# Feed-forward tiles, key and query stages and row statistics at other steps of a software-pipelined Flamingo block, with its maximum jobs in another order

## What is computed

```
x = x + tanh(g_xattn) * attention(layernorm(x), ctx, ctx)     # 16 heads of 32, masked: ki <= qi + 1601 - 512
x = x + tanh(g_ffn)   * ffn(layernorm(x))                     # both sides rounded to fp8 by rows
  ffn: g, u = q(x) @ Wgate.T, q(x) @ Wup.T   (width 1408, by down_reorder_index)
       t = silu(g) * u ;  y = q(t) @ Wdown.T
```

## Time and profile before

| | us |
|---|---|
| median of 3 runs (1201.39 to 1202.09) | 1202.0 |
| the profiled execution | 1203.17 |
| its span | 1201.4 |
| PE busy | 1003.3 (84%) |
| DVE busy | 855.0 (71%) |
| ACT busy | 652.1 (54%) |
| POOL busy | 327.4 (27%) |

### The profile page before, as it was taken

One profiled execution on the slowest core, in us unless ns is written; L12 is line 12 of the kernel. 1 busy time (PEld: TensorE's weight loads), 2 busy tenths in 40 slices (PEclk: granted clock), 3 DMA queues, 4 the chain that ended last, 5 costly groups with the idle time before them and its releaser, 6 DMA issues.

```text
span 1201.4 us, 18722 instructions
## 1 busy us (share of the span) xinstructions
PE 1003.3 (84%) x6651; PEld 392.1 (33%) x6666; DVE 855.0 (71%) x1406; ACT 652.1 (54%) x1326; POOL 327.4 (27%) x334
## 2 busy tenths in 40 slices
PE   4698878888989989999998989999899999884353
PEld 1233323333333333333333333333333333332131
DVE  8878877887678586767877686857776766244873
ACT  2155756675656565655656465656565556561321
POOL 3013323332012232322322131222222222233452
PEclk9898988999999999989999999999999999996776
DMA  7933322322842211126413112127311110000000
GB/s 151 178 79 97 116 54 63 90 72 53 124 80 57 62 26 49 33 59 99 95 37 91 36 28 64 29 58 112 74 31 29 28 36 2 9 1 9 9 10 17
DMA packets 155108, 70.53 MB, mean 59 GB/s; under 512 B 111032, under 2 KB 142856, under 8 KB 155016
## 3 DMA queue, kind: packets, MB, share of 16 engines
q1 hardware_dynamic: 153256, 63.57, 24.7%
q0 software_dynamic: 1760, 5.77, 1.7%
HBM read 39.08 MB, written 4.19 MB: 36 GB/s over the span
## 4 chain that ended last, share of the span: by engine, by line
PE 54%; DVE 24%; issue 12%; POOL 5%; ACT 5%; DMA 0%; POOLq 0%; SPq 0%; DVEq 0%; ACTq 0%
PE ps L804 17%; DVE mch L996 11%; PE ps L780 11%; PE ps L824 6%; PE ps L724 6%; PE ps L843 3%; DVE ff L922 2%; PE ps L728 2%; PE ps L750 1%; DVE ff L918 1%; ACT pr L589 1%; DVE ff L914 1%; DVE ff L1074 1%; PE ps L752 1%; POOL t_q L409 1%
## 5 line engine op out<-in xcount | busy, mean ns | idle before, releaser
L589 ACT ACTIVATE pr<-ps 128x512 f32<-128x512 f32 (+4 forms) x832 | 396.8, 528 | 275.5 <-PE ps L786 141.3
L996 DVE TENSOR_REDUCE mch<-ps 128x2 f32<-128x1024 f32 (+4 forms) x416 | 433.4, 1056 | 85.2 <-PE ps L724 58.1
L804 PE MATMUL ps<-pr,vf 128*33 128x512 f32 (+4 forms) x1664 | 392.0, 552 | 0.0
L780 PE MATMUL ps<-qst,kst 97*64 97x512 f16 (+4 forms) x1600 | 257.1, 381 | 13.9 <-ACT pr L589 11.5
L724 PE MATMUL ps<-kTh,qTh 32*128 32x512 f16 (+4 forms) x832 | 158.0, 378 | 68.1 <-DVE mch L996 38.9
L724 PEld LDWEIGHTS ps<-kTh,qTh 32*128 32x128 f16 x832 | 39.9, 92 | 292.1 <-DVE mch L996 110.8
L780 PEld LDWEIGHTS ps<-qst,kst 97*64 97x64 f16 (+1 forms) x1600 | 76.4, 111 | 114.6 <-ACT pr L589 53.7
L804 PEld LDWEIGHTS ps<-pr,vf 128*33 128x33 f32 (+1 forms) x1664 | 88.2, 115 | 61.1 <-issue 10.2
L421 POOL TENSOR_TENSOR xs<-xs,upd 128x256 f32<-128x256 f32 x32 | 23.3, 728 | 282.0 <-DVE upd L1039 282.0
L1074 DVE SCALAR_TENSOR_TENSOR ff<-ps,scs,wsb 128x352 f32<-128x352 f32 x56 | 32.7, 583 | 70.1 <-PE ps L824 69.8
L824 PE MATMUL ps<-wgu,t_T 128*128 128x352 bf16 x448 | 79.6, 323 | 2.5 <-ACT t_T L610 1.5
(11 more groups left out here) (146 smaller groups left out, 1164.1 us busy)
## 6 DMA issues: line engine op xcount, KB each, us to landing
kst<-kTh SPq DMA_DIRECT2D x128, 100.1 KB, 2.2
ksrc<-in_ctx SPq DMA_DIRECT2D x16, 768.0 KB
vf<-in_ctx SPq DMA_DIRECT2D x48, 256.0 KB, 4.5
kst<-kTl SPq DMA_DIRECT2D x64, 100.1 KB, 2.2
xs<-in_x SPq DMA_DIRECT2D x16, 256.0 KB, 3.8
qst<-qTh SPq DMA_DIRECT2D x128, 32.0 KB, 1.9
out<-xs SPq DMA_DIRECT2D x16, 256.0 KB, 2.0
ff<-in_L_ffn_w_down SPq DMA_DIRECT2D x4, 704.0 KB, 5.2
```

Source lines behind the costliest of these rows:

```text
L589: nc.scalar.activation(pr[0:kn, n % NP, q0:S], ps[0:kn, j, q0:S], ACT.Exp, scale=SCALE).then_inc(ex_done, 1)
L780: last = nc.tensor.matmul(ps[a:e, j, q0:S], kst[s][0:ST, r, k0 + a:k0 + e], qst[s][0:ST, r, q0:S], start=True, stop=(t < DT))
L804: nc.tensor.matmul(ps[64 * j:64 * j + VW, 2 + pp % 2, q0:S], vf[0:kn, t, h, :], pr[0:kn, n % NP, q0:S], start=(t == 0), stop=(t == NT - 1) ...
L996: nc.vector.tensor_reduce(mch[:, qt, 2 * hp:2 * hp + 2, c], both[:, :, 0:k1 - k0], AX.X, ALU.max).then_inc(dve_free, 1)
```

## The change

The order of the maximum jobs: the four rests of a pair come together as jobs 4 to 7 (449, 193, 321, 65 wide), that is at steps 24, 25, 0, 1 and 11, 12, 13, 14. The stage jobs go from steps 5, 7, 13 to 10, 13, 19. Tiles 0 to 11 start at step 15 of a group instead of 9, so offset k stands at step (15 + k) mod 26: norming 15, row scale 16, rounding 18 and 19, rows turn 20, up turns 22, 24, 0, 2, hidden chunks 25, 1, 3, 5, hidden scale 5, scaling 6, the three wide DVE operations 7, 8, 9, POOL 10, hidden turn 12, down turn 14. The norming of queries is spread over steps 7, 8, 9 and 16, one group ahead of where it was needed; the copies of group 2 leave the preparation. The statistics of x stand one tile a step in steps 12 to 15, their rest in 17; those of the attended rows in 6 to 9, their rest in 10, POOL's power in 11, the shift in 12 (the last batch's stay together behind the loop). On SP four of the eight value loads go ahead of `put_heads(gg + 2, 0)`.

```diff
--- before.py
+++ after.py
@@ -50,10 +50,13 @@
 
     chunks = []
     for hp in range(PAIRS):
+        full, last = [], []
         for qt in range(QT):
             end = NEAR + P * (qt + 1)
             for c in range((end + 511) // 512):
-                chunks.append((hp, qt, c, 512 * c, min(512 * c + 512, end)))
+                k0, k1 = 512 * c, min(512 * c + 512, end)
+                (full if k1 - k0 == 512 else last).append((hp, qt, c, k0, k1))
+        chunks += full[0:4] + [last[2], last[0], last[1], last[3]] + full[4:]
     CH = len(chunks)
     assert CH == STEPS
 
@@ -64,7 +67,8 @@
         gg, j = divmod(at + AHEAD, STEPS)
         return (gg + 1, j) if gg + 1 < GALL else None
 
-    STAGE_AT, SUMS_AT, SUF_AT, FINISH_AT, MT_AT = {5: 1, 7: 2, 13: 0}, 7, 11, STEPS - AHEAD, 23
+    STAGE_AT, SUMS_AT, SUF_AT, FINISH_AT, MT_AT = {10: 1, 13: 2, 19: 0}, 7, 11, STEPS - AHEAD, 23
+    NORM_AT, X_STATS_AT, OUT_STATS_AT = (7, 8, 9, 16), (12, 13, 14, 15), (6, 7, 8, 9)
     PARTS = (1, 2, 0)
     LAST = GALL * STEPS
     TILES = B * QT
@@ -72,7 +76,7 @@
 
     def tile_base(n):
 
-        return STEPS * (n + NG) + 9 if n < TILES - QT else LAST + 7 + 13 * (n - TILES + QT)
+        return STEPS * (n + NG) + 15 if n < TILES - QT else LAST + 7 + 13 * (n - TILES + QT)
 
     END = tile_base(TILES - 1) + TILE_STEPS
 
@@ -350,11 +354,14 @@
                     load_keys(sp, gg + 3)
                 if gg >= NG + 1:
                     put_out(sp, gg - NG - 1)
+                if g == NG - 1 and b + 1 < B:
+                    for t in range(4):
+                        load_values(sp, b + 1, t)
                 if gg + 2 < GALL:
                     sp.wait_ge(dve_free, dve_count["stage", gg + 2, 0])
                     put_heads(sp, gg + 2, 0)
                 if g == NG - 1 and b + 1 < B:
-                    for t in range(8):
+                    for t in range(4, 8):
                         load_values(sp, b + 1, t)
                 if gg + 1 < GALL:
                     put_shift(sp, gg + 1)
@@ -423,6 +430,8 @@
 
         def row_std(pool, b):
             pool.wait_ge(var_ready, b + 1)
+            if b >= 1:
+                pool.wait_ge(xl_ready, QT * NG * b)
             nc.gpsimd.tensor_tensor(rstd[:, :], ve[:, :], half[:, :], ALU.pow).then_inc(rstd_ready, 1)
 
         def out_row_std(pool, b):
@@ -486,8 +495,10 @@
                 gg, u = divmod(at, STEPS)
                 if turned_at(at) is not None:
                     add_update(pool, turned_at(at))
-                if at >= NG * STEPS and gg % NG == 0 and u == 6:
+                if NG <= gg < GALL and gg % NG == 0 and u == 11:
                     out_row_std(pool, gg // NG - 1)
+                if at == LAST + 6:
+                    out_row_std(pool, B - 1)
                 if gg < GALL - NG and gg % NG == 1 and u == 18:
                     row_std(pool, gg // NG + 1)
                 if gg + 1 < GALL and u == MT_AT:
@@ -548,13 +559,13 @@
             to = (qTh, kTh, kTh)[part]
             nc.scalar.copy(to[:, gg % 2, c0:c1], slot(("stage", gg, part))[:, 0:c1 - c0]).then_inc(hi_done, 1)
 
-        def norm_cols(act, gg):
+        def norm_cols(act, gg, tiles):
 
             b, g = divmod(gg, NG)
             act.wait_ge(nmr_ready, b + 1)
             if gg >= 1:
                 act.wait_ge(st_mm, 3 * gg)
-            for qt in range(QT):
+            for qt in tiles:
                 nc.scalar.activation(xlg[:, qt, :], xs[:, b % 3, qt, g * P:(g + 1) * P], ACT.Identity, bias=nmr[:, qt:qt + 1],
                                      scale=rstd[:, qt:qt + 1]).then_inc(xl_ready, 1)
 
@@ -640,15 +651,14 @@
             act.wait_ge(gate_mm, 1)
             nc.scalar.activation(tg[:, :], ps[:, 0, 0:2], ACT.Tanh).then_inc(gate_th, 1)
             stage_high(act, 0, 1)
-            norm_cols(act, 0)
+            norm_cols(act, 0, range(QT))
             stage_high(act, 0, 2)
             stage_high(act, 0, 0)
-            norm_cols(act, 1)
+            norm_cols(act, 1, range(QT))
             shift_copy(act, 0)
             masked_weight(act, 0)
             for part in PARTS:
                 stage_high(act, 1, part)
-            norm_cols(act, 2)
             for at in range(END):
                 gg, u = divmod(at, STEPS)
                 if gg + 2 < GALL and u in STAGE_AT:
@@ -660,8 +670,8 @@
                 if gg + 1 < GALL and u == MT_AT:
                     shift_copy(act, gg + 1)
                     masked_weight(act, gg + 1)
-                if u == MT_AT + 2 and gg + 3 < GALL:
-                    norm_cols(act, gg + 3)
+                if gg + 2 < GALL and u in NORM_AT:
+                    norm_cols(act, gg + 2, [NORM_AT.index(u)])
                 for n, k in tiles_at(at):
                     if k == 0:
                         norm_rows(act, n)
@@ -946,9 +956,10 @@
             rows, m, _ = weight_job(j)
             add_rounder(s, rows, m).then_inc(w_added, 1)
 
-        def row_stats(dve, s, b, to):
-            for qt in range(QT):
-                s.step(nc.vector.bn_stats(stat[:, qt, :], xs[:, b % 3, qt, :]))
+        def row_stats(s, b, qt):
+            s.step(nc.vector.bn_stats(stat[:, qt, :], xs[:, b % 3, qt, :]))
+
+        def row_variance(dve, s, to):
             s.settle()
             dve.nop(nofuse=True)
             for qt in range(QT):
@@ -956,16 +967,21 @@
             s.settle()
             return nc.vector.tensor_scalar(ve[:, :], to[:, :, 1], EPS, None, ALU.add)
 
-        def norm_stats(dve, s, b):
-            for qt in range(QT):
-                dve.wait_ge(x_in[qt], 16 * (b + 1))
+        def norm_stats(dve, s, b, qt):
+            dve.wait_ge(x_in[qt], 16 * (b + 1))
+            row_stats(s, b, qt)
+
+        def norm_variance(dve, s, b):
             if b >= 2:
                 dve.wait_ge(rstdf_ready, b - 1)
-            row_stats(dve, s, b, mv).then_inc(var_ready, 1)
-
-        def out_stats(dve, s, b):
+            row_variance(dve, s, mv).then_inc(var_ready, 1)
+
+        def out_stats(dve, s, b, qt):
             dve.wait_ge(xs_done, (b + 1) * NG * PAIRS)
-            row_stats(dve, s, b, mvf).then_inc(varf_ready, 1)
+            row_stats(s, b, qt)
+
+        def out_variance(dve, s, b):
+            row_variance(dve, s, mvf).then_inc(varf_ready, 1)
 
         def norm_shift(dve, b):
 
@@ -1109,7 +1125,9 @@
             nc.vector.memset(kst[1][ST - 1:ST, :, :], 1.0).then_inc(ones_in[1], 1)
             dve.wait_ge(consts, 15)
             s = Steps(dve)
-            norm_stats(dve, s, 0)
+            for qt in range(QT):
+                norm_stats(dve, s, 0, qt)
+            norm_variance(dve, s, 0)
             norm_shift(dve, 0)
             for part in PARTS:
                 stage_low(dve, 0, part)
@@ -1133,12 +1151,23 @@
                     suffix_weigh(dve, gg)
                 if max_job_at(at) is not None:
                     max_reduce(dve, *max_job_at(at))
-                if at >= NG * STEPS and gg % NG == 0 and u == 6:
-                    out_stats(dve, s, gg // NG - 1)
-                if at >= NG * STEPS and gg % NG == 0 and u == 7:
-                    out_shift(dve, gg // NG - 1)
-                if gg < GALL - NG and gg % NG == 1 and u == 18:
-                    norm_stats(dve, s, gg // NG + 1)
+                if NG <= gg < GALL and gg % NG == 0:
+                    if u in OUT_STATS_AT:
+                        out_stats(dve, s, gg // NG - 1, OUT_STATS_AT.index(u))
+                    if u == 10:
+                        out_variance(dve, s, gg // NG - 1)
+                    if u == 12:
+                        out_shift(dve, gg // NG - 1)
+                if at == LAST + 6:
+                    for qt in range(QT):
+                        out_stats(dve, s, B - 1, qt)
+                    out_variance(dve, s, B - 1)
+                if at == LAST + 7:
+                    out_shift(dve, B - 1)
+                if gg < GALL - NG and gg % NG == 1 and u in X_STATS_AT:
+                    norm_stats(dve, s, gg // NG + 1, X_STATS_AT.index(u))
+                if gg < GALL - NG and gg % NG == 1 and u == 17:
+                    norm_variance(dve, s, gg // NG + 1)
                 if gg < GALL - NG and gg % NG == 1 and u == 19:
                     norm_shift(dve, gg // NG + 1)
                 for n, k in tiles_at(at):
```

## The result

The changed kernel takes 1183.07 us, the median of 4 runs (1181.31 to 1184.63), against 1201.76 for the kernel before on the same chip: ratio 0.983, 95% interval 0.9808 to 0.9852. It is 18.7 us faster; the forecast was 2.1 us faster, and the time lies outside the range (1189 to 1211). The profiled execution took 1184.63 us, span 1182.9.

The account below looks back on a forecast made before the run. PE, busy 84% of the span, was taken as the bound. Terms -2.6 + 0 - 2.7 - 2.5 - 4.7 + 5.0 + 10.4 - 5.0 = -2.1 took 1203.2 us to 1201.1 (median 1199.9), range 1189 to 1211.

Parts of the forecast that it names:

- (8): Low-clock stretches: six after steps 0 to 2 go, two come in behind late shift rows; four less, -5.0 us.
- (2): PE stalls step by step in feed-forward groups: 5.9 us against 6.2, -0.3 a group, -2.7 us over nine groups.
- (7): Short maximum jobs in short steps: take DVE's shortage out of steps 24 to 1 and 11 to 14; no separate size.
- (1): Feed-forward tiles six steps later: two up turns leave the main loop, -2.6 us; part behind the loop 0.
- (3): Query norming spread one tile per step: removes one wait of about 0.5 us in groups 0 to 4, -2.5 us.
- (4): Row statistics of x spread over steps 12 to 17: -0.6 each in groups 5 and 9, -3.5 in group 1; -4.7 us.
- (5): Finished rows' statistics in steps 6 to 10: delay the suffix job by 2.5 us in groups 8 and 12; +5.0 us.
- (6): Query stage in step 19, SP's queue: shift row late behind value loads, scores stand 6.4, 2.0 and 2.0 us; +10.4 us.
- The clock rival: New stalls and narrow middle steps draw three more low-clock stretches: +3.8 instead of -5.0, time 1208.7 us; chance 0.28.
- the early row: Shift row on SP's queue is not late for the next group's scores: 10.4 us less, 1189.5 us; chance 0.17.
- everything re-forms: Stalls come from DVE's total work and return elsewhere, statistics eat the saved bursts: 1202.0 us; chance 0.10.

Follow-up runs that it names:

- the best kernel: Changed kernel with the old order of maximum jobs and, on SP, the shift row first, then all late value loads, then the second heads: 1151.03 us, ratio 0.9583.
- first experiment: Changed kernel with the maximum jobs put back in their old order, nothing else undone: 1176.60 us, ratio 0.9757.

## Why the prediction was wrong

The mechanisms were nearly all right; it was wrong in sizes, and the 16.6 us missed are 7.5 of clock, 7.7 of stalls and 5.8 in two groups that the sum left out, less some 4 us in small terms that went the other way.

**The failed step is (8), the clock.** That "those of steps 13 to 15 stay" was wrong. In groups 5 to 15 there were 14 low stretches, 7 after steps 0 to 2 and 7 after steps 13 to 15. The first went as foreseen: all seven are gone, and two came in behind late shift rows (groups 8 and 12), as the forecast had it. Of the second only two are left. Ten fewer x 1.25 = -12.5, where four fewer and -5.0 stood. Two runs bear it out: doubled matmuls in steps 13 and 14 alone win 11.5 us with a group at full clock unchanged, and in the best kernel the tiles at their old steps bring low time into every group from 5 on. What keeps the clock at 2.4 GHz in steps 12 to 15 of the changed kernel is not one edit. The new order alone nearly does it (17.1 us low in groups 5 to 15 instead of 47.8), and the best kernel, with the later tiles and the old order, has none. Which dense work takes over in the changed kernel was not separated further. The rule in the Trainium skill (TensorE: Matmul & The Clock Gate, HAM oscillation) that PE must have no long idle gaps does not account for these falls: the longest wait in the stretch at 440.70 above is 0.57 us. The prediction's sentence that by that rule no stretch would be low before the end left out its own wait of 4.87 us, in which a low stretch begins (178.6).

**(2), the stalls, was mis-sized too:** 1.2 us a group, where 0.3 stood, so -10.4 instead of -2.7 over nine groups. By its steps: step 13's 0.98 and step 23's 0.4 came as written; steps 2 and 14, with 0.45 and 0.3, had none; step 8 had 0.38 instead of 1.0, the suffix job 0.67 instead of 1.0, steps 19 to 21 1.15 instead of 1.85. DVE was run as a queue that never catches up, and it does catch up. The sum was wrong in itself, too: with the 0.4 us of small gaps the new stalls written out add up to 6.4, not 5.9, so by its own count a group would have lost 0.2 us. Which edit wins what here depends on the rest: the placement of tiles, stages and statistics gives 2.0 us a full-clock group with the old order (62.8 to 60.8, first experiment), the order takes 0.9 of them back. (7) "inside (2)" hid that the order has a price of its own: +0.9 us a group and 1.7 more in groups 8 and 12 (statistics 2.5 instead of 0.8) in this placement, besides 1.1 us (59.8 against 58.7) of preparation.

**Left out:** groups 14 and 15, which have no stages left to make. PE's waits in group 15 went from 5.1 to 2.1 us, and PE's unbusy time in group 14 from 4.0 to 1.2 (54.02 - 52.83). That is -5.8 us, and the old tile steps bring most of it back.

**The other steps.** (1) Right: the up turn's matmuls in the loop went from 384 to 368, two turns, though they leave group 4 and not the end; the part behind the last scores got +0.8 for 0 (+3.0 to the first up turn, -2.4 by its clock). (3) Wrong: -2.5 foreseen, nothing measured. (4) Right in sign: group 1's stall fell from 4.87 to 1.70 (foreseen about 1), groups 5 and 9 lost 1.1 and 1.3 us net of clock and stalls, -0.6 each foreseen; in the best kernel the edit is worth 13.1 us with the clock. (5) Right with this order, 2.4 to 2.5 a group, and 0.8 with the old one. (6) Right: +5.7, +3.5 and +2.6, sum 11.8, where 10.4 stood; the small row did wait behind the loads, and moving it ahead took all three away. From the end of the heads to the row's use it was 9.6 us in group 3 (312.79 to 322.37), where 9.5 stood, but more of it is issue (5.31 for the four loads, against 3.5) and less is landing. The rule in the Trainium skill (DMA: Bandwidth & Descriptors, Two DMAs through the same engine are not ordered) is that within one queue of an engine descriptors start in order. This trace agrees with it without proving it: the row was in use 4.18 us after its issue, against at most 3.05 with no load right ahead of it.

The ledger for groups 5 to 15: clock 34.2 us less low time at 0.37 (group 11 against 6 of before, 2.5 / 6.8) to 0.43, -12.6 to -14.7; steady groups -10.4; groups 14 and 15 -5.8; groups 5 and 9 -2.4; groups 8 and 12 +4.8; groups 7 and 11 +6.1. Sum -20.3 to -22.4, measured -20.8. Up to group 5 the late row (+5.7) ate what the rest gave.

The clock rival had the sign wrong, and the early row did not happen. That everything re-forms was wrong for the waits; but edits do replace each other: the order gives 20.9 us alone and costs 6.5 in the changed kernel. That both it and the later tiles fill the same weak steps, and can win them only once, is argued from these two numbers, not shown.

## What to carry to other kernels

Where PE is some 85% busy and its clock falls now and then, find the few steps with short jobs, turns and waits after which it falls, and put dense work there: it can be worth as much as the waits themselves (14.1 us for the clock in one run here, 10.4 for the stalls of the full-clock groups), and a duplicate matmul shows in one run how much. Put a small transfer that the next step waits for ahead of large loads in its queue. Time the edits of a bundle one by one with and without each other: one that wins alone can lose in company.

## What the runs showed of the hardware

- More matmuls made the kernel faster (11.5 us), as they kept the grant at 2.4 GHz; a us at 1.2 GHz cost 0.37 to 0.43 us in the kernel before. With the best kernel's tiles at their old steps the loss was larger than that, and not accounted for.
- The clock fell with no long wait before it: in the 3.4 us before three falls PE had been busy 2.14, 2.20 and 2.53 us, and the longest wait in the last of them was 0.57 us. It did not fall after other stretches with PE busy 2.11 and 1.76 us, so the busy time alone does not tell.
- Four 256 KB loads issued in a bunch took 5.31 us of SP's time, and the scores waited 5.67 us for a 4 KB row behind them; with the row ahead of the loads they did not wait.
